# One segment maximum over four score banks, behind both halves of the band, in a two-layer transformer kernel

## What is computed

```python
q = (hidden_states @ w_q).reshape(B, S, H, Dh)
k = (hidden_states @ w_k).reshape(B, S, H, Dh)
v = (hidden_states @ w_v).reshape(B, S, H, Dh)
allowed = local | dil          # same segment of 64, or distance a multiple of 4 and at most 256
scores = jnp.einsum('bqhd,bkhd->bhqk', q, k) * scaling + mask[None, None]
attn = jax.nn.softmax(scores.astype(jnp.float32), axis=-1).astype(q.dtype)
out = jnp.einsum('bhqk,bkhd->bqhd', attn, v).reshape(B, S, H * Dh)
x = x + out @ w_o
```

## Time and profile before

| | |
|---|---|
| median of 3 executions | 480.09 us (478.1, 480.09, 482.02) |
| span of the profiled execution | 478.9 us; the page gives no time for it beside the span |
| TensorE busy | 448.3 us, 94% of the span |
| VectorE busy | 403.7 us, 84% |
| ScalarE busy | 331.6 us, 69% |
| GpSimd busy | 297.0 us, 62% |
| head, loop, drain, tail | about 24 to 62, 62 to 304, 304 to 330, and from 318 to 478.9 us |

### The profile page before, as it was taken

One profiled execution on the slowest core, in us unless ns is written; L12 is line 12 of the kernel. 1 busy time (PEld: TensorE's weight loads), 2 busy tenths in 40 slices (PEclk: granted clock), 3 DMA queues, 4 the chain that ended last, 5 costly groups with the idle time before them and its releaser, 6 DMA issues.

```text
span 478.9 us, 17292 instructions
## 1 busy us (share of the span) xinstructions
PE 448.3 (94%) x6440; PEld 351.4 (73%) x6440; DVE 403.7 (84%) x1368; ACT 331.6 (69%) x972; POOL 297.0 (62%) x501
## 2 busy tenths in 40 slices
PE   6899989999999999999999999999878879989995
PEld 4678768888887887887888788877544746558674
DVE  5987759987998898889898688897999998998674
ACT  3477858878777768768778767865653687986433
POOL 4134638777577668668668567548478897572222
PEclk9899999999999999999999999999998999999999
DMA  6278682355344344345464645443000000000002
GB/s 219 110 215 245 166 270 51 73 114 118 74 95 94 73 93 95 72 94 116 87 135 100 138 96 106 83 87 67 1 0 0 2 0 1 1 2 1 1 0 89
DMA packets 136099, 40.54 MB, mean 85 GB/s; under 512 B 104976, under 2 KB 131024, under 8 KB 136016
## 3 DMA queue, kind: packets, MB, share of 16 engines
q1 hardware_dynamic: 135440, 38.38, 34.8%
q10 hardware_dynamic: 576, 1.05, 0.6%
HBM read 29.44 MB, written 9.96 MB: 82 GB/s over the span
## 4 chain that ended last, share of the span: by engine, by line
PE 59%; SPq 9%; POOL 9%; DVE 8%; DMA 6%; ACT 5%; issue 3%; ACTq 0%; POOLq 0%; DVEq 0%
PE psum L416 10%; PE psum L458 9%; PE psum L1181 5%; PE psum L478 5%; PE psum L492 4%; PE psum L504 4%; PE psum L489 4%; PE psum L397 4%; SPq L285 3%; PE psum L1176 3%; PE psum L399 2%; PE psum L398 2%; DMA st<-w_rows_dram 2%; DMA w_rows_dram<-st 2%; POOL rs L1899 2%
## 5 line engine op out<-in xcount | busy, mean ns | idle before, releaser
L942 POOL TENSOR_SCALAR pband<-pband,fac 128x192 f32<-128x192 f32 x256 | 104.1, 427 | 85.6 <-DVE fac L758 85.5
L562 ACT ACTIVATE pband<-pband,st 128x192 f32<-128x192 f32 x256 | 113.2, 448 | 0.1
L706 DVE CUSTOM_DVE_ANT_0 pband<-psum,band_mask 128x192 f32<-128x192 f32 x256 | 76.2, 353 | 1.0 <-PE psum L416 0.9
L416 PE MATMUL psum<-keys,q_class 64*64 64x192 f32 (+2 forms) x1536 | 66.5, 275 | 0.5 <-issue 0.5
L458 PEld LDWEIGHTS psum<-ident,pband 128*128 128x128 f32 x384 | 45.2, 141 | 21.6 <-issue 13.6
L416 PEld LDWEIGHTS psum<-keys,q_class 64*64 64x64 f32 x1536 | 57.6, 133 | 3.4 <-issue 2.6
L458 PE MATMUL psum<-ident,pband 128*128 128x128 f32 x384 | 53.2, 274 | 2.6 <-DVE pt L767 2.6
L562 ACT ACTIVATION_READ_ACCUMULATOR pband<-pband,st 128x1 f32 x256 | 49.5, 193 | 0.0
L924 POOL COPY keys<-k_rows 128x512 f32<-128x512 f32 x32 | 36.2, 1132 | 19.0 <-issue 10.7
L767 DVE COPY pt<-psum 128x512 f32<-128x512 f32 x64 | 43.7, 683 | 2.1 <-PE psum L458 1.9
L932 POOL COPY q_class<-q_rows 128x512 f32<-128x512 f32 x32 | 36.3, 1134 | 11.3 <-ACT q_rows L602 11.3
(11 more groups left out here) (221 smaller groups left out, 1103.6 us busy)
## 6 DMA issues: line engine op xcount, KB each, us to landing
v_rows_dram<-arena SPq DMA_DIRECT2D x32, 256.0 KB, 3.5
v_both<-v_rows_dram SPq DMA_DIRECT2D x32, 256.0 KB, 3.7
v_seg<-v_rows_dram SPq DMA_DIRECT2D x64, 128.0 KB, 3.6
v_side<-v_rows_dram SPq DMA_DIRECT2D x96, 64.0 KB, 2.6
w_rows_dram<-st SPq DMA_DIRECT2D x64, 8.0 KB, 2.9
st<-w_rows_dram SPq DMA_DIRECT2D x64, 8.0 KB, 2.5
arena<-_attn_hidden_states_dram SPq DMA_DIRECT2D x4, 256.0 KB, 3.6
out_dram<-x SPq DMA_DIRECT2D x4, 256.0 KB, 2.5
```

Of the source, the lines that this page charges most:

```text
L416: return pe.matmul(bank[2 * r + head][rows, at:at + y.shape[1]], x, y, start=True, stop=True, skip_group_check=True)
L562: act.activation(x, x, ACT.Exp, bias=mine[:, head:head + 1], scale=-1.0, accum_out=mine[:, 2 + head:3 + head]).then_inc(s_exp, 1)
L706: dve.tensor_tensor_reduce(pband[:, G % P_SLOTS, c, head, :], bank[2 * r + head][:, at:at + BAND], band_mask[:, (0, 1, 1, 2)[w], SEG * (1 ...
L942: pool.tensor_scalar(x, x, fac[:, F % 2, 1, c, head:head + 1], 1.0, ALU.mult, ALU.mult).then_inc(s_scaled, 1)
```

## The change

`seg_max` loses its argument r. One reduction takes the minimum over all four banks (128x512), then two subtractions (128x256 each) follow, one per pair of banks, each with its own count on `s_seg`. It stands behind `band_max(G, 0)` and `band_max(G, 1)` everywhere; before, its first half stood behind the first half of the band or ahead of it, and its second half ahead of the second half of the band. TensorE's, ScalarE's, GpSimd's and SyncE's lists and all their waits are the same.

```diff
-    def seg_scores(r):
-
-        return psum[:, 2 * r:2 * r + 2, SEG_AT:512].rearrange("p h (k x) -> p h k x", x=SEG)
+    def seg_scores():
+
+        return psum[:, 0:4, SEG_AT:512].rearrange("p (r h) (k x) -> p r h k x", r=2, x=SEG)
...
-            def seg_max(G, r):
+            def seg_max(G):
...
-                dve.wait_ge(s_score, 2 * G + r + 1)
-                top = st[:, G % P_SLOTS, 0, 0, 2 * r:2 * r + 2, 0:2].rearrange("p k h -> p h k")
-                dve.tensor_reduce(top, seg_scores(r), AX.X, ALU.min).then_inc(s_segmax, 1)
-                dve.wait_ge(s_segmax, 2 * G + r + 1)
-                dve.tensor_tensor(pseg[:, G % P_SLOTS, 2 * r:2 * r + 2, :, :].rearrange("p k h x -> p h k x"),
-                                  top.unsqueeze(3).to_broadcast([P, 2, 2, SEG]), seg_scores(r),
-                                  ALU.subtract).then_inc(s_seg, 1)
+                dve.wait_ge(s_score, 2 * G + 2)
+                top = st[:, G % P_SLOTS, 0, 0, :, 0:2].rearrange("p (r k) h -> p r h k", r=2)
+                dve.tensor_reduce(top, seg_scores(), AX.X, ALU.min).then_inc(s_segmax, 1)
+                dve.wait_ge(s_segmax, G + 1)
+                mine = pseg[:, G % P_SLOTS, :, :, :]
+                for r in range(2):
+                    dve.tensor_tensor(mine[:, 2 * r:2 * r + 2, :, :].rearrange("p k h x -> p h k x"),
+                                      top[:, r, :, :].unsqueeze(3).to_broadcast([P, 2, 2, SEG]), seg_scores()[:, r, :, :, :],
+                                      ALU.subtract).then_inc(s_seg, 1)
...
                 band_max(t - 2, 0)
-                seg_max(t - 2, 0)
                 even_turned(t - 5, 2)
-                seg_max(t - 2, 1)
                 band_max(t - 2, 1)
+                seg_max(t - 2)
                 seg_sums(t - 2)
```

More of the change, by code:

```diff
@@ L862, in _ @@
             take_values(1); moments(2); take_lo(1); normalise(2); take_values(3); split_v(1); moments(3)
[L863 to L869, removed]
+            take_values(5); take_lo(2); normalise(3); take_values(7); band_max(0, 0); take_values(9)
+            take_lo(3); band_max(0, 1); seg_max(0); take_values(11); seg_sums(0); band_max(1, 0)
+            take_values(13); band_max(1, 1); seg_max(1); take_values(15); seg_sums(1); take_values(17)
+            differences(0); take_values(19); factors(0); band_max(2, 0); take_values(21)
+            take_values(23); band_max(2, 1); seg_max(2); seg_sums(2); take_values(25); take_values(27); differences(1)
+            take_values(29); factors(1); band_max(3, 0); take_values(31); even_turned(0, 0)
+            even_turned(0, 2); band_max(3, 1); seg_max(3); seg_sums(3)
             for t in range(FIRST_STEP, DRAIN):
@@ L894, in _ @@
              xr, k1, k2, o0, o) = tail_vector(dve)
-            differences(29); even_turned(28, 0); factors(29); band_max(31, 0); even_turned(28, 2); seg_max(31, 0)
-            seg_max(31, 1); accumulate(27); band_max(31, 1); clear(); seg_sums(31); accumulate(28); differences(30)
+            differences(29); even_turned(28, 0); factors(29); band_max(31, 0); even_turned(28, 2); accumulate(27)
+            band_max(31, 1); seg_max(31); clear(); seg_sums(31); accumulate(28); differences(30)
             even_turned(29, 0); factors(30); x1(0); bn0(0); ag0(0); even_turned(29, 2); even_turned(30, 0); qx0(0)
```

## The result

The changed kernel takes 482.86 us (median of 18 executions, 481.24 to 484.86), the kernel before on the same chip 480.32 us (18 executions, 476.25 to 482.31). The ratio is 1.0062 with a 95% interval of 1.0042 to 1.0082: by it slower by 3.0 us (2.0 to 3.9), while the two medians lie 2.5 us apart. A ratio leaves out the executions that took over 1.5% longer than the fastest of the same kernel; here there are none. The forecast was 483.6 us and +3.5 us.

The account below looks back on a forecast made before the run. TensorE, busy 224.99 of 226.00 us, was taken to bound the loop. Head 1.7, loop 0 and drain 1.8 us gave +3.5 us on the median of 480.09, so 483.6 us, range 480.0 to 487.8.

Parts of the forecast that it names:

- The segment part's cost on VectorE: VectorE, each unit: 1.58 us falls to 1.40, saving 5.8 us over 32, all spent waiting before `seg_sums`.
- D: Rival: the four-bank reduction far above its 0.84 us bound; at 1.5 us, +5 us more, 489 us; chance 0.02.
- The loop: 0: Loop, 74 to 300 us: next scores keep cover in all units but one; loss 0, at most 0.1 us.
- Unit 26: Loop: the one unit without cover, its next scores beginning exactly 2.86 us after the band's first half ends.
- The head: 0.9 + 2.4 + 0.4 - 2.0 = +1.7: Head: TensorE stalls at units 0, 2 and 3, less a vanished 2.00 us wait; ends 0.9 and 3.7 us.
- The third term: Head, unit 3: copy L578 behind `seg_exps` ends at 64.25, TensorE wanted it at 63.96: 0.4 us.
- The signal from VectorE to TensorE: Head, unit 0: delay between the freeing subtraction and TensorE's scores, estimated at 0.1 us.
- The give-back: Head: TensorE's 2.00 us wait before the transposes at 69.30 vanishes; SyncE's queue slips only by 0.9 us.
- The drain: +1.8: Drain, units 30 and 31: `output(27)` 0.8 us late, `output(28)` 2.5, `x1(0)` at 323.25 instead of 321.42; ends 0.5 and 2.5.
- A: Rival: stalls of head and drain fall into other waits; +0 to +1, 480.1 to 481 us; chance 0.14.
- B: Rival: the exchange moves with TensorE, so the 2.00 us wait stays; 485.6 us, up to 487; chance 0.25.
- C: Rival: VectorE's list paces the loop, so the 5.8 us saving counts; 474.3 us; chance 0.04.

Follow-up runs that it names:

- e1: Kernel before with the change in loop units 4 to 28 alone, head and units 29 to 31 as before: 480.93 us, ratio 0.9996.
- e4: Changed kernel with the one reduction over four banks put ahead of the band's second half, in head, loop and drain: 480.23 us, ratio 0.9996 to before.
- f3: Changed kernel with unit 2 of the head alone in the old order: 482.03 us, ratio 1.0056 to the kernel before.
- f1: Kernel before with `fetch_statistics(2)` moved ahead of four stores of values in SyncE's queue: 480.04 us, ratio 0.9997.
- f4: Changed kernel with `take_out(28)` and `odd_turned(29, 1)` ahead of `seg_exps(31)` in ScalarE's list: 481.76 us, ratio 1.0043 to before.
- e2: Changed kernel with the head as before, loop and drain changed: 482.43 us, ratio 1.0053 to before.
- g1: Kernel before with `fetch_statistics(2)` and `load_wo()` moved behind `store_v(24)` in SyncE's queue: 480.8 us, ratio 0.9965.
- e3: Changed kernel with the drain (units 29 to 31) as before, head and loop changed: 481.53 us, ratio 1.0027 to before.
- f2: Changed kernel with `fetch_statistics(2)` moved ahead of four stores of values in SyncE's queue: 482.8 us, ratio 1.0066 to before.
- g3: Kernel before with the joined reduction ahead of the band's second half, `fetch_statistics(2)` and `load_wo()` behind `store_v(24)`: 482.88 us, ratio 0.9950.
- g2: Changed kernel with `fetch_statistics(2)` and `load_wo()` moved behind `store_v(24)` in SyncE's queue: 484.86 us, ratio 1.0041 to before.

## Why the prediction was right, and where its sizes were off

**The result as a whole.** 483.6 us was forecast, 482.86 measured; +3.5 us forecast, +3.0 (2.0 to 3.9) measured; within 1%, as held likeliest. The terms stand up one by one below, so the agreement isn't luck; that they sum so closely to 3.5 leans on a pair of profiles that carry some tenths of noise each.

**The segment part's cost on VectorE.** 0.69 us for the reduction and 5.8 us saved, all of it spent waiting. Measured 689 ns on average, 5.5 us less busy time, and 5.6 us more idle time before `seg_sums`. Right. D (a reduction far over its bound) falls with it. By the Trainium skill, "Perfetto Trace Analysis", Optimizing Scalar/DVE Operations, grouping pays on a saturated engine. The runs agree: VectorE, at 198 of 226 us, isn't saturated, and e1 and e4, which keep the grouping, gain nothing by it. The other half of the rule, that breaking up may let work finish sooner, isn't what decides here: e4 breaks nothing up and loses nothing.

**The loop: 0.** Right, by e1 and by 224.78 of 226 us. Unit 26, which I had at its limit (scores exactly 2.86 us behind the count's start), is at it:

```profile
273.69 0.75 DVE L722 TENSOR_TENSOR pseg<-st,psum 128x256 f32<-128x256 f32 x2
...
274.26 0.38 PE L416 MATMUL psum<-keys,q_class 64*64 64x192 f32 x2
```

The first of the two subtractions ends at 273.69 + 0.42 = 274.11, and the scores follow 0.15 us later, the same distance as at the stalls of the head (31.39 to 31.54; 50.64 to 50.78). So the subtraction released them there too, just in time for TensorE not to fall idle. In the other units of the loop the distance is 0.3 us or more in this profile: nothing was lost, but unit 26 had no cover left.

**The head: 0.9 + 2.4 + 0.4 - 2.0 = +1.7.** Measured as idle time of TensorE 1.01, 2.34, 0.16, and the 2.00 gone: +1.5; from unit 0's band to unit 6's it took 1.6 us longer than before (61.90, 60.30) and 1.3 longer than in e4 (60.62). The third term looks too large by its idle time and isn't: between these rows TensorE took 65.89 - 58.72 = 7.17 us before and takes 67.73 - 60.19 = 7.54, so 0.37 us later for 0.4 forecast. Before:

```profile
65.89 0.50 PE L397 MATMUL psum<-xn_hi,w_hi 128*128 128x512 f32 x1
```

After:

```profile
60.19 1.14 PE L458 MATMUL psum<-ident,pband 128*128 128x128 f32 x8
...
67.73 0.50 PE L397 MATMUL psum<-xn_hi,w_hi 128*128 128x512 f32 x1
```

The signal from VectorE to TensorE, put at 0.1 us, takes 0.15. The give-back is right in size, and f3 shows its mechanism from the other side. The step beneath it was off: SyncE's queue was to slip by unit 0's 0.9 us. Its DMA issue (L307) that stood at 63.58 stands at 61.75, and the whole execution was 2.09 us ahead by then, so it slipped 0.3 us. The prediction named only the statistics as paced by the queue; f1 shows that w_o's load behind them is as late.

**The drain: +1.8.** Measured +1.95. `output(27)` waits 0.72 us (0.8 forecast), `output(28)` 1.67 more: 2.4 us in all, 2.5 forecast. That the second wait comes from the order of ScalarE's list is shown by f4; that this order isn't the whole cause is shown there too. `x1(0)` was forecast at 324.9 and stands at 322.99, since this execution began 2.09 us earlier; 322.99 + 2.09 = 325.1.

**The rivals.** A (nothing lost) falls by the interval, which begins at 1.0042, and by e2: the drain's 1.95 us isn't swallowed. B (the 2.00 us wait stays, over 1%) falls by the trace at 68.53 and by the interval, which ends at 1.0082. C (faster) falls by e1 and e4.

**Open.** Where g1 gains its 0.35%; whether the head or the drain costs more, and how much of the drain's loss hangs on what; and what the wait near 269 us depends on (below).

## What to carry to other kernels

Where a producer writes banks that aren't doubled, the read that frees them goes first, and joining two reads is free only as long as it doesn't push them behind other work: here the same joined reduction cost 0.6% behind the band and nothing measurable ahead of it. A dense loop can hide such a move entirely, so read the head and the drain by themselves, where the producer's list between two uses of a bank is short. And look at what the late engine would have waited for next: a new stall can be paid back there, and a wait taken away there may only uncover the next thing in the same queue.

## What the runs showed of the hardware that I had not expected

**The clock falls around a wait of TensorE, in some executions and not in others.** In e3 it fell with the stall at `scores(3, 0)`, in the profile after, with the same stall at the same place, it didn't. TensorE's windows in e3, with the granted clock third from the end:

```profile
48.00:51.60 3.60, 1.51 (x6) 0.90 (x6) 2.71 (x11) 1.71 (x7) 3.06 (x7) 1.00 0.82 272
51.60:55.10 3.50, 3.25 (x43) 2.96 (x44) 1.13 (x3) 2.86 (x10) 0.00 (x0) 0.51 0.66 143
55.10:58.60 3.50, 3.30 (x15) 2.42 (x15) 1.76 (x4) 1.70 (x4) 1.09 (x1) 1.00 0.56 109
```

From 51.6 to 55.1 us it is at about 0.50, the 1.2 GHz level, and at 1.00 on both sides. Each of the fourteen profiles has one wait of TensorE of 1.8 us or more between 24 and 80 us; with eight of them such a stretch of about 3.4 us began, from 0.3 us before the wait's end to 1.3 us after it (e1, e2, e3, f1, f2, f3, f4, g3). The kernel before had one behind a wait of 1.87 us at 12.56 us, as e2 and e3 had behind 2.67 and 2.56; the eleven other profiles, after among them, waited 0.95 to 1.35 us there, and none had one. At half the clock 3.4 us of dense matmuls lose at most 1.7 us. Over the 18 executions of the changed kernel the span is 481.2 to 482.8 us where the mean clock was 0.990 or 0.991, and 479.5 and 480.1 us where it was 1.000; but in between, at 0.993 to 0.998, it is 479.7 to 483.1, so the clock isn't the only thing that varies. So one profile against one profile can hide an effect of 3 us, as here; a pair of stretches that no such fall touches, or many executions, is what can be compared. Stalls of 2 us thus carry an uncertain surcharge, on either kernel: before, its 2.00 us wait; after, the 2.34 us one. That no fall followed some waits of the same length stays unexplained.

**The exchange through DRAM varies.** Kernels with the same lists of TensorE and VectorE in the loop waited for it near 270 us not at all (e3, f4), for 0.23 (e1), 1.20 (e2), 1.22 (after) and 1.27 us (f3), and with another order in SyncE's queue 200 us earlier 0.69 (f2) and 1.64 us (g2); the old lists for 0.56 (before) and, with that other order, 1.11 (f1) and 2.15 us (g1). A difference of 1 us in a wait of this kind, in one profile each, is no evidence for or against an edit.
